# Taking the second normalisation's deviation from the first one's variance, and a new order of all steps

## The reference

```
x = layernorm(x + attention(x))
x = layernorm(x + decoder(x, context))      # cross attention, self attention, GELU feed-forward;
                                            # each is h -> (h - mean) * rsqrt(var + 1e-5) * gain + shift
x = layernorm(x + mixture(x))
# mixture: scores = x @ centroids.T, expert = argmax(scores), alpha = sigmoid(best score)
# ys = x + relu(LN(x) @ W1[expert].T + b1) @ W2[expert].T + b2, with LN(x) = (x - mu) * rsqrt(var + 1e-5) * gamma + beta
# out = alpha * ys + (1 - alpha) * x
```

## Time and profile before

| | |
|---|---|
| median of three runs | 392.32 us |
| the profiled execution | 392.81 us, of which its span (first to last instruction) 390.8 us |
| mean granted TensorE clock | 0.993 of full speed |
| PE busy | 377.9 us, 97% of the span |
| DVE busy | 262.0 us, 67% |
| ACT busy | 242.0 us, 62% |
| POOL busy | 126.7 us, 32% |

### The profile page before, as it was taken

One profiled execution on the slowest core, in us unless ns is written; L12 is line 12 of the kernel. 1 busy time (PEld: TensorE's weight loads), 2 busy tenths in 40 slices (PEclk: granted clock), 3 DMA queues, 4 the chain that ended last, 5 costly groups with the idle time before them and its releaser, 6 DMA issues.

```text
span 390.8 us, 10252 instructions
## 1 busy us (share of the span) xinstructions
PE 377.9 (97%) x3630; PEld 319.9 (82%) x3630; DVE 262.0 (67%) x904; ACT 242.0 (62%) x814; POOL 126.7 (32%) x250
## 2 busy tenths in 40 slices
PE   8999999999999999999999999999999998999992
PEld 8886788888888787888888888878889897989671
DVE  5469768787768768687787854468778884334531
ACT  1117866897897888998989899598332050422230
POOL 5223116113114213032033411342456445723331
PEclk9999999999999999999999999999999999999997
DMA  6980160221212012161000001937010429999400
GB/s 210 294 285 4 50 208 18 79 86 25 62 40 64 24 39 57 43 250 37 3 2 27 24 4 56 388 127 329 2 39 28 142 78 396 405 431 426 176 13 32
DMA packets 14277, 48.88 MB, mean 125 GB/s; under 512 B 2048, under 2 KB 8672, under 8 KB 12304
## 3 DMA queue, kind: packets, MB, share of 16 engines
q1 hardware_dynamic: 12256, 35.58, 26.5%
q0 software_dynamic: 1824, 12.35, 7.7%
q10 hardware_dynamic: 144, 0.26, 0.2%
HBM read 41.44 MB, written 4.91 MB: 119 GB/s over the span
## 4 chain that ended last, share of the span: by engine, by line
PE 81%; DVE 5%; ACT 4%; DMA 4%; issue 3%; POOL 1%; POOLq 0%; DVEq 0%; ACTq 0%
PE bank_pt L708 15%; PE bank_out L546 12%; PE bank_scores L692 7%; PE bank_out L730 6%; PE bank_out L532 5%; PE bank_out L572 5%; PE bank_out L539 5%; PE bank_scores L561 4%; DMA arena<-x_slots 4%; PE bank_pt L744 4%; PE bank_out L601 4%; PE bank_out L754 3%; PE bank_scores L698 2%; ACT arena L1332 1%; PE bank_out L553 1%
## 5 line engine op out<-in xcount | busy, mean ns | idle before, releaser
L1321 ACT ACTIVATE arena<-arena,negmaxc 112x375 f32<-112x375 f32 x128 | 76.9, 604 | 10.0 <-DVE negmaxc L1066 9.7
L1341 ACT ACTIVATE arena<-bank_pt 125x448 f32<-125x448 f32 (+1 forms) x128 | 65.4, 542 | 19.2 <-PE bank_pt L708 17.2
L1066 DVE CUSTOM_DVE_ANT_0 arena<-bank_scores,arena 112x375 f32<-112x375 f32 x128 | 65.8, 541 | 13.1 <-PE bank_scores L698 9.1
L708 PE MATMUL bank_pt<-ident,arena 112*125 112x112 f32 (+1 forms) x512 | 70.4, 271 | 0.0
L708 PEld LDWEIGHTS bank_pt<-ident,arena 112*125 112x125 f32 (+1 forms) x512 | 62.6, 175 | 7.5 <-issue 0.9
L546 PE MATMUL bank_out<-arena 128*112 128x256 f32 (+1 forms) x224 | 57.1, 383 | 0.1
L1437 POOL TENSOR_TENSOR vareps<-meanvar,scal 112x1 f32<-112x1 f32 (+1 forms) x47 | 9.6, 203 | 116.6 <-DVE meanvar L931 109.4
L1332 ACT ACTIVATE arena<-bank_scores,negmaxs 112x112 f32<-112x112 f32 x128 | 43.6, 354 | 3.1 <-DVE negmaxc L1066 0.9
L546 PEld LDWEIGHTS bank_out<-arena 128*112 128x112 f32 (+1 forms) x224 | 37.2, 181 | 7.5 <-issue 1.9
L1382 ACT ACTIVATE arena<-bank_scores,consts 128x128 f32<-128x128 f32 x64 | 18.2, 368 | 37.5 <-PE bank_scores L561 36.9
L561 PE MATMUL bank_scores<-arena 128*128 128x128 f32 x256 | 30.1, 276 | 1.3 <-issue 1.2
(11 more groups left out here) (191 smaller groups left out, 662.3 us busy)
## 6 DMA issues: line engine op xcount, KB each, us to landing
arena<-moe SPq DMA_DIRECT2D x8, 2048.0 KB, 10.0
arena<-ctxT SPq DMA_DIRECT2D x8, 375.0 KB, 3.1
arena<-mask SPq DMA_DIRECT2D x8, 164.1 KB, 3.2
x_slots<-arena SPq DMA_DIRECT2D x8, 130.0 KB, 2.4
arena<-x_slots SPq DMA_DIRECT2D x8, 130.0 KB, 2.2
arena<-weights SPq DMA_DIRECT2D x2, 512.0 KB, 8.1
arena<-rows SPq DMA_DIRECT2D x1, 1024.0 KB, 13.2
arena<-weights SPq DMA_DIRECT2D x1, 1024.0 KB, 5.7
```

Source lines behind the costliest of these rows:

```text
L708: last = nc.tensor.transpose(dst[0:kp, j * S:(j + 1) * S], probs[0:S, (n % 2) * HG + j, c * kp:(c + 1) * kp], ident[0:S, 0:S])
L1066: v.tensor_tensor_reduce(out=probsC[0:S, i % (2 * HG)], in0=score_bank[j][0:S, 0:KX], in1=masks[0:S, u % 2], scale=-1.0, scalar=3.0e38, op ...
L1321: a.activation(probsC[0:S, i % (2 * HG)], probsC[0:S, i % (2 * HG)], ACT.Exp, bias=negmax["c"][0:S, u, at:at + 1], scale=-1.0, accum_out=s ...
L1341: a.activation(probsT[0:kp, n % RT, c], pt_bank[PT[stage, i] % RP][0:kp, 0:HG * S], ACT.Copy).then_inc(pt_free, 1)
```

## The change

The column `MEAN` of the scattered rows becomes `DEV`. DVE's part of `zn` (statistics over the 256 numbers of y) is gone. POOL's part now needs only `meanvar`, `vareps` and `rstd` of the slot that `zf` took: it writes sqrt(v + e) to `DEV` and rsqrt(v (1 + e) + e*e) to `RSTD`, with three instructions in place of two. Who normalises a tile multiplies by both numbers instead of subtracting one and multiplying by the other. The scatter waits for `zb` by name, since `zn` no longer does. A slot of `zf` is used again only after POOL's `zn` has read it. The step list has the same 663 steps in another order, from the first line to the last.

```diff
--- before.py
+++ after.py
@@ -35,7 +35,7 @@
 EXPERT_AT = [t if t < MIXED_AT else t - 1 for t in range(E + 1)]
 PW = 3 * D + F
 XW = D + 4
-ALPHA, TOKEN, MEAN, RSTD = range(D, XW)
+ALPHA, TOKEN, DEV, RSTD = range(D, XW)
 NR = 6
...
 ORDER = (
-    "aqk*2 as aqk at aw as av cv as ay at ck*2 ab av at as ax av cq aqk ay at cm*3 qk as cm ab ck*2 qk cm as ct cm*2 cv cm ay ct*2 cm "
...
-    "sqk ct sm cn ct sn pv ct qk ct pr sm sv ct sx ct sx qk st sm f1 sb sx st sm qk pv st f1 sm cy qk sy f1 sn cb f1 cx sn f2 st pr sqk "
-    "st f1 zf pr zx sm qk pv zb pv f1 sb sx sy qk sm st sc sb f2 qk st sm sx f1 zf sv zx zn f1 rk sm sc zb qk st f2 sn*2 zf zn st f2 "
-    "pr*2 pv*2 zb f1 zf zx*2 al f1 sc sy rk zb al f1 rk sb zn sc f1 sx f2 zn zf al f2 zx al zb f1 rk sc zn zf f1 rk al zb zn f2 wm zx "
-    "room wm zf wm zx sc zb wm en sc rk al wm ei rk first zn first al first tot ei first*3 en first*10 ")
+    "aqk*2 as aqk at aw as av cv ay at as ck ab ck av at as ax av cq aqk cm qk cm*3 ay as ck cm qk av ab ct cm cv cm*2 ct cv ax ct cm "
...
+    "cm*2 sv pr ct sm cn pv st ct qk pr sn sm sb sx ct sv ct sx qk st sm f1 st qk sm pv st f1 sy qk sm cy cb f1 sx f1 sn cx sn f2 pr*2 "
+    "sqk st*2 sm pv qk zf pv f1 sb zx f1 sm qk sy f2 st sm sx qk zn sv zf sb f1 zn sc zx f1 sx qk sm sn st sc f2 zb sn rk st*2 zf f2 "
+    "pr*2 zb pv*2 zf zb f1 rk sy al zx zn al f1 zx sb zn sc f1 sc rk f1 zb sx al f2 zf zn f2 zx zb al f1 rk sc zf al f1 rk zb f2 room "
+    "wm zn zx wm*2 zf zx en sc wm sc wm al ei rk*2 first zn first tot al first*2 ei first en first zb first*10 ")
...
@@ -257,7 +257,7 @@
         sums = {k: sb("sums" + k, [128, B, h]) for k, h in (("a", 1), ("c", H), ("s", H))}
         recips = {"a": sb("recipsa", [128, B, 1]), "c": sb("recipsc", [128, 2, 128]), "s": sb("recipss", [128, 2, 128])}
         stats = sb("stats", [128, NR, 6])
-        stats5 = sb("stats5", [128, 6])
+        x5_var = sb("x5_var", [128, 2, 1])
         meanvar = sb("meanvar", [128, NR, 2])
         vareps = sb("vareps", [128, NR, 1])
         rstd = sb("rstd", [128, NR, 1])
...
@@ -917,7 +917,8 @@
                     was, wi = next(s for s, n in OPENED.items() if n == k - NR)
                     dve.wait_ge(norm_done, FINISHED[FINISHES[was], wi] + 1)
                     if was == "zf":
-                        assert STEPS.index(("sc", wi)) < STEPS.index((stage, i))
+                        assert max(STEPS.index(("sc", wi)), STEPS.index(("zn", wi))) < STEPS.index((stage, i))
+                        dve.wait_ge(x5_rstd, 2 * (wi + 1))
                         dve.wait_ge(out_full, OUT["zx", wi] + 1)
                     if was in ("cy", "sy"):
                         dve.wait_ge(out_full, OUT[was[0] + "x", wi] + 1)
@@ -1083,14 +1084,6 @@
                                            ALU.mult, ALU.add).then_inc(norm_done, 1)
                     dve.wait_ge(norm_done, FINISHED[stage, i] + 1)
                     take_stats(k, BLOCK)
-                elif stage == "zn":
-
-                    dve.wait_ge(norm_done, FINISHED["zb", i] + 1)
-                    if i:
-                        dve.wait_ge(x5_stats, i)
-                    link(v.bn_stats(stats5[:, :], x1[:, i]))
-                    linked()
-                    v.bn_aggr(xrows[:, i, MEAN:MEAN + 2], stats5[:, :]).then_inc(x5_stats, 1)
                 elif stage == "sc":
 
                     src, k = full(slot), OPENED["zf", i]
@@ -1144,8 +1137,8 @@
 
                     dve.wait_ge(tile_in[1] if i else early_in, 16)
                     x = early_x[i]
-                    v.tensor_scalar(early_xn[i], x[:, 0:D], x[:, MEAN:MEAN + 1], x[:, RSTD:RSTD + 1],
-                                    ALU.subtract, ALU.mult).then_inc(early_normed, 1)
+                    v.tensor_scalar(early_xn[i], x[:, 0:D], x[:, DEV:DEV + 1], x[:, RSTD:RSTD + 1],
+                                    ALU.mult, ALU.mult).then_inc(early_normed, 1)
             dve.wait_ge(out_free, N_OUT)
 
             def place_rest():
@@ -1205,12 +1198,12 @@
                     dve.wait_ge(t_xT_full, j - 1)
                 m = mixed(j)
                 if m is None:
-                    v.tensor_scalar(xsn[:, j % 2], x[:, 0:D], x[:, MEAN:MEAN + 1], x[:, RSTD:RSTD + 1], ALU.subtract, ALU.mult)\
+                    v.tensor_scalar(xsn[:, j % 2], x[:, 0:D], x[:, DEV:DEV + 1], x[:, RSTD:RSTD + 1], ALU.mult, ALU.mult)\
                         .then_inc(t_normed, 1)
                 else:
                     dve.wait_ge(params_in[m % 3], 16 * (m // 3 + 1))
-                    v.scalar_tensor_tensor(xsn[:, j % 2], x[:, 0:D], x[:, MEAN:MEAN + 1], params[:, m % 3, 0:D],
-                                           ALU.subtract, ALU.mult).then_inc(t_gained, 1)
+                    v.scalar_tensor_tensor(xsn[:, j % 2], x[:, 0:D], x[:, DEV:DEV + 1], params[:, m % 3, 0:D],
+                                           ALU.mult, ALU.mult).then_inc(t_gained, 1)
                     dve.wait_ge(t_gained, m + 1)
                     v.scalar_tensor_tensor(xsn[:, j % 2], xsn[:, j % 2], x[:, RSTD:RSTD + 1], params[:, m % 3, D:2 * D],
                                            ALU.mult, ALU.add).then_inc(t_normed, 1)
@@ -1473,17 +1466,20 @@
                         pool.wait_ge(x1_moved[i - 2], 16 * len(MOVES[i - 2]))
                     g.tensor_tensor(moved_x1[0:S, i % 2], x1[0:S, i], R["fobe"], ALU.add).then_inc(x1_biased, 1)
                 elif stage == "zn":
-                    pool.wait_ge(x5_stats, i + 1)
-                    g.tensor_tensor(xrows[:, i, RSTD:RSTD + 1], xrows[:, i, RSTD:RSTD + 1], scal[:, 0:1], ALU.add)\
-                        .then_inc(x5_vareps, 1)
-                    pool.wait_ge(x5_vareps, i + 1)
-                    g.tensor_tensor(xrows[:, i, RSTD:RSTD + 1], xrows[:, i, RSTD:RSTD + 1], scal[:, 1:2], ALU.pow)\
-                        .then_inc(x5_rstd, 1)
+                    k = OPENED["zf", i]
+                    pool.wait_ge(rstd_ready, k + 1)
+                    if i >= 2:
+                        pool.wait_ge(x5_rstd, 2 * (i - 1))
+                    g.tensor_scalar(x5_var[:, i % 2], meanvar[:, k % NR, 1:2], 1.0 + EPS, EPS * EPS, ALU.mult, ALU.add).then_inc(x5_varied, 1)
+                    g.tensor_tensor(xrows[:, i, DEV:DEV + 1], vareps[:, k % NR], rstd[:, k % NR], ALU.mult).then_inc(x5_rstd, 1)
+                    pool.wait_ge(x5_varied, i + 1)
+                    g.tensor_tensor(xrows[:, i, RSTD:RSTD + 1], x5_var[:, i % 2], scal[:, 1:2], ALU.pow).then_inc(x5_rstd, 1)
                 elif stage == "al":
 
                     if i == 0:
                         pool.wait_ge(zero_in, 16 * TILES)
-                    pool.wait_ge(x5_rstd, i + 1)
+                    pool.wait_ge(x5_rstd, 2 * (i + 1))
+                    pool.wait_ge(norm_done, FINISHED["zb", i] + 1)
                     pool.wait_ge(alphaed, i + 1)
                     pool.wait_ge(placed, i + 1)
                     if i >= BLOCKS - LATE:

```

More of the change, by code:

```diff
@@ L323, in decoder_layer @@
             "dve_chain pool_chain").split()]
-        (e_chain, p_chain, x5_stats, x5_vareps, x5_rstd, best_ready, best_scaled, exped, alphaed, picked, placed, scattered, totals, more_placed,
+        (e_chain, p_chain, x5_varied, x5_rstd, best_ready, best_scaled, exped, alphaed, picked, placed, scattered, totals, more_placed,
          more_scattered, moe_in0, t_normed, t_xT_full, t_xT_ready, t_gained, t_rows_full, t_rows_ready, t_hid_full, t_hid_ready,
@@ L328, in decoder_layer @@
          early_in, early_normed, counted) = [sem(n) for n in (
-            "e_chain p_chain x5_stats x5_vareps x5_rstd best_ready best_scaled exped alphaed picked placed scattered totals more_placed "
+            "e_chain p_chain x5_varied x5_rstd best_ready best_scaled exped alphaed picked placed scattered totals more_placed "
             "more_scattered moe_in0 t_normed t_xT_full t_xT_ready t_gained t_rows_full t_rows_ready t_hid_full t_hid_ready "
```

## The result

The changed kernel takes 396.03 us (median of 20 executions, 393.33 to 401.67) against 392.26 us for the kernel before (20 executions, 391.3 to 392.97). It is slower, where 391.8 us was forecast, and outside the range of 389.8 to 394.0. The profiled execution, 393.84 us with a span of 392.1, is one of the shortest of the twenty and shows only part of the loss; the rest is seen in the experiments' profiles.

The account below looks back on a forecast made before the run. PE was taken to bound the kernel, with DMA level within a few tenths in the tail. Terms of 0.3 (first `f2`) and 0.25 (last scatter) made 0.55 us off the 392.32 us median: 391.8 us, range 389.8 to 394.0.

Parts of the forecast that it names:

- the term of 0.25: End of the list: the last scatter and SP's loads behind it start 0.25 us earlier, leaving 0.25 us gained at the end.
- The other term, 0.3 at the first `f2`: First `f2`: 0.3 of PE's 0.65 us wait for the previous piece's GELU is won back; ends 0 and 0.65.
- DVE's 0.62 us a block: DVE, 268 to 315 us: loses seven statistics pairs, 4.3 us in all, giving PE nothing until the list's end.
- POOL's `zn`: POOL's normalisation step costs 0.9 to 1.4 us, taken as 1.1 instead of 0.85; only the last lies on a path.
- PE 0.8 earlier at the tail: End of the list: PE reaches the tail 0.8 us earlier, ends 0.2 and 1.2, turning into longer tail waits.
- The wait before the second L781: End of the list: PE's 0.46 us idle for the second expert tile's rows ends.
- The last scatter 0.1 to 0.5 closer behind `f2` 6: Sign of being right, on POOL at the list's end: the last scatter follows the last `f2` by 0.1 to 0.5 us less.
- The tail's waits longer: Sign of being right: PE's tail waits at L581 and L833 grow, since DMA does not come much earlier.
- B: Rival, dense stretch: ACT holds PE up, 0.65 us per place; three places give 393.8 us; chance 0.18.
- C: Rival, last block: POOL and DVE collide; if DVE waits up to 0.567 us, 392.3 us; chance 0.15 together with D.
- D: Rival, list's end: first expert tile's normalisation blocks DVE if rows land late, about 0.5 us, 392.3 us; 0.15 with C.
- A: Rival, tail: scatter and PE both move 0.8 to 1.2 us earlier, with all 0.65 of `f2`, 390.6 us; chance 0.25.

Follow-up runs that it names:

- the formula alone: Kernel before with the new deviation formula (DVE's statistics gone, three POOL instructions) and the old step order: 397.56 us, ratio 1.0133.
- the pad: Two powers (1.10 us) on POOL ahead of its first `x_more` scatter: 1.0016 added to the new formula in old order, 1.0025 added to the changed kernel.
- all seventeen profiles: One profiled execution each of the kernel before, the changed kernel, its repeat and the experiments' other kernels; their ratios to before run from 0.9980 to 1.0151.
- the second one: Profile of the changed kernel run once more with nothing altered: 397.43 us, ratio 1.0107.
- `zn` 6 early with rows 5 ahead of expert 7: Changed kernel with block 6's `zn` ahead of block 5's `al`, and tile 5's rows loaded before expert 7's weights: 392.15 us, ratio 1.0006.
- `zn` 6 early: Changed kernel with block 6's `zn` ahead of block 5's `al`, so POOL's instructions leave the gap between its last two scatters: ratio 1.0025.

## Why the prediction was wrong

*The step that failed* is "So it starts 0.2 us earlier, call it 0.25 with the gaps. The loads of 320.01 follow at 319.76", the term of 0.25 in the sum. The last scatter came 1.01 us later and SP's loads at 321.23. Of the 1.01, 0.90 is the later last `f2`: the prediction compared positions within the end of the list and took the time at which PE reaches it from the first `f2`, but the waits between 250 and 302 us set it back. The other 0.11 is the end itself. The scatter of block 5, for which 0.45 was taken off, starts only 0.08 earlier behind the last `f2` (12.92 in place of 13.00), and the two scatters stand 0.19 further apart, where 0.25 was added. The other term, 0.3 at the first `f2`, gave 0.02.

*What the sum did not have* is the `x_more` scatter. The prediction listed what stands behind DVE's missing pair on PE (`tot`) but not what stands behind `tot` on POOL. It also read the tail as an amount of bytes, in which 0.25 us earlier is 0.25 us gained. The experiments show that which queue starts first is worth 4.6 us with the formula alone (1.0133 to 1.0016 by the pad) and 2.3 to 3.2 us in the changed kernel, many times the terms that were added up. That SP's first load comes first, or at most 0.10 us behind POOL's scatter, tells the streams of all seventeen profiles apart: 1.24 to 1.46 MB on the one side, 0.75 to 1.14 from 0.21 us on.

*What else is left.* With the pad, the changed kernel is still 1.0025 [1.0009, 1.0042], about 1 us, and SP's loads are 1.38 us later there (321.39). It is of the size of the 0.9 us that PE itself loses before the last `f2`. That the late start costs this much is inferred; no run moved it alone.

*Step by step.* First `f2`, 0.3 us back: wrong, 4.09 us in place of 4.11, the lower end of its range. DVE's 0.62 us a block worth nothing to PE: right. POOL's `zn`: 0.97 us from its first start to its last end (316.68 to 317.65) where 1.1 was taken (0.85 before). The form with two constants, unknown then, takes 0.18, inside its bounds. PE 0.8 earlier at the tail: wrong, 2.16 later in the profiled execution and 0.66 later in the second one, which has no low clock at 316 us (322.31); so the low clock is worth some 1.5 of the 2.16. From the last `f2` on, that second profile is 0.37 us shorter (19.58 in place of 19.95), inside the term's ends of 0.2 and 1.2, but less than the 0.9 lost before. The wait before the second L781: gone as forecast, but moved to `tot`, which had been expected to be ready. The last scatter 0.1 to 0.5 closer behind `f2` 6: wrong, 0.11 further. The tail's waits longer: wrong in this profile, right in others, for a reason that the prediction did not have.

*The rivals.* B had the right sign, and its mechanism is not shown: it would be PE waiting behind ACT, and the only such idle time is the old one. What ended the short waits inside PE's busy time between 250 and 302 us stays open, so B is not excluded for these 0.9 us; they are not the 4 us that the formula alone costs in the old order. C: POOL and DVE do collide again, POOL and then DVE here,

```profile
307.80 0.48 POOL L1430 TENSOR_TENSOR vareps<-meanvar,scal 128x1 f32<-128x1 f32 x1 [1.57 <-DVE meanvar L932]
...
309.00 0.48 POOL L1473 TENSOR_SCALAR x_var<-meanvar 128x1 f32<-128x1 f32 x1
```

```profile
307.74 0.48 DVE L1016 SCALAR_TENSOR_TENSOR arena<-arena,meanvar 128x256 f32<-128x256 f32 x1
...
308.95 0.48 DVE L1083 SCALAR_TENSOR_TENSOR arena<-arena,rstd,xrows 128x256 f32<-128x256 f32 x1
```

and POOL alone pays: 0.48 against 0.19 when free, DVE's are not longer than in the earlier trace rows. D did not occur. A is the mirror of what happened: the tail does move by more than the scatter does, in the other direction.

## What to carry to other kernels

Removing work from an engine that bounds nothing is not free: look for what it releases, down to the DMAs, and for what those meet. Where two queues start within half a microsecond of each other, write down which is first before and after the change. A small transfer behind large ones in one queue, due just when another queue fills with large packets, is a cliff; put it ahead of the large ones, or test it by holding the other queue back.

## What had not been expected of the hardware

- Two issues 0.1 to 0.5 us apart decide how much SP's queue moves in 4 us: 1.24 to 1.46 MB with the load first or at most 0.10 us behind, 0.75 to 1.14 with the scatter first by 0.21 us or more. Why a few 130 KB scatters hold 2 MB loads back so much, while the total rate falls too, no run settles.
- Between two queues that both had work, the packets were shared evenly (199 and 194 in 6 us, 199 and 187 in the formula alone), not the bytes (2.41 and 0.21 MB).
- After an idle time of PE of 3.98 us the granted clock was at the lower level, 0.57 on average over the next 4 us, which adds 1.3 us to sixteen records. The same fall at 316 us followed an idle time of 0.46 us in two profiles (the changed kernel's, and that of `zn` 6 early with rows 5 ahead of expert 7); with `zn` 6 early alone the same idle time of 0.46 us stands in the same place and the clock stays at its upper level. No run settles why.
